# Layer 0 of a four-layer graph network: the x tiles turned on TensorE instead of loaded turned

## The chip, the cores and the metric

The kernel runs on one core of a Trainium2 chip. The metric is the device time of one launch in microseconds (us), as a median of several runs; lower is better.

## The reference

The input x is 128 graphs of 64 nodes with 512 features, in float32; adj is one 64x64 matrix of zeros and ones that all graphs share. Four layers follow one another, each as `x = layernorm(x + layer(x))`. Only layer 0 is touched here:

```python
Wi, Wj = (W[:, :Din], W[:, Din:])
mi = jnp.einsum('bkd,od->bko', x, Wi)
mj = jnp.einsum('bkd,od->bko', x, Wj)
a = adj.astype(x.dtype)
deg = a.sum(axis=1)
out = deg[None, :, None] * (mi + b) + jnp.einsum('ij,bjo->bio', a, mj)
```

Layer 1 is a graph attention with four heads, an output attention and a feed-forward part; layers 2 and 3 are graph attentions with one head.

## The kernel before, in words

The 8192 rows of x are cut into T = 64 tiles of 128 rows, two graphs each. Layer 0 is a first block of the program that runs over the 64 tiles; its result goes to a scratch tensor in HBM, and layer 1, then layers 2 and 3, are later blocks that this change leaves alone.

TensorE contracts over partitions, so x must stand with its features on the partitions. The host hands the kernel x twice: as it is, and a second tensor `in_x_turned` in which each tile is already transposed by blocks of 128x128. SyncE loads both for each tile: `xt` (128 rows by 512 features, two buffers) and `xf`, in the profile `x0f` (features on the partitions, two buffers).

Precision comes from splitting: each float32 operand becomes a high part (cast to fp32r) and a low part (the rest), and each product is three matmuls, high by high, high by low and low by high. For one tile t the engines do this, each in its own fixed order, with semaphores between them:

- ScalarE (ACT): `x_hi(t+1)` casts `xf` into `x0T_hi` (L644); then `wj_hi(t)` (L651) casts the product wj out of PSUM; then `normalise(t-1)` writes the layer's output (L656) and issues its store (L659).
- VectorE (DVE): `x_lo(t+1)` (L698), `xf` minus `x0T_hi`; `wj_lo(t)` (L719); in the first 48 tiles one dot product for the attention vectors of later layers (L727), which needs `v_stage` and `a_pair` from HBM; `z(t)` in two steps (L737, L741); statistics (L284, L291).
- TensorE (PE): `products(t)`: 12 matmuls into `wj_psum`, 12 into `wi_psum`, both through `product` (L47), then 2 into `nb_psum` with the adjacency (L774, L775), which wait for `wj_lo(t)`.
- GpSimd (POOL): `xb(t)` = `xt` + `db` (L607), the small steps of the norm (L295, L298, L302, L307), and between them the splitting of layer 1's weights from `stage` into `big_hi` and `big_lo` (L595, L600), one block for two tiles, loaded from its own DMA queue (L591).
- SyncE (SP): in each step, in this order: at the start of a group of 8 tiles the two loads of `a_pair` (L547), in each even tile that of `v_stage` (L551), then a wait for `xT_lo_ready` and the load of `xf` for tile t+3 (L554), then a wait for `xb_ready` and the load of `xt` for tile t+2 (L558).

At the start SP loads `xf[0]`, the adjacency, the first two pieces of layer 0's weight, the bias, `xf[1]` and both `xt` (L524 to L536). Each further piece of the weight is loaded once DVE has made the low part of an earlier one. The one transpose on PE in layer 0 is that of the adjacency (L779).

Later blocks transpose 128x128 blocks on PE too: `pe_turn` of the head attention (L250), `turn_att` (L1973) and `turn_h1` (L1986), four transposes each, into a PSUM bank.

Of the kernel before, what the change touches and what calls it, by code (L numbers as in the profile page):

```python
# [394 lines left out]
            nc.gpsimd.tensor_tensor(self.shift, self.less, self.rstd, ALU.mult).then_inc(self.shift_ready, 1)  # L395


def gnn_stack_kernel(nc, x, x_turned, adj, W0T, b0, Wh, ah, Wo, ao, w1, b1, w2, b2, gamma, beta,
                     W2, a2s, a2d, W3, a3s, a3d, out):
    B, N, _ = x.shape  # L400
    T = B * N // P
# [13 lines left out]
    with ExitStack() as top:  # L415
# [29 lines left out]
        with ExitStack() as ctx:  # L445
# [3 lines left out]
            def sem(n):  # L449
                return ctx.enter_context(nc.semaphore(n))  # L450

            XR, UN = 2, 4
            GROUP = 2 * KC
            WP = 2
            w0 = (sb("w0_hi", [P, 2 * KC, D], F32R), sb("w0_lo", [P, 2 * KC, D], F32R))
# [3 lines left out]
            a_pair = sb("a_pair", [P, 2, D])  # L459
            v_sums = sb("v_sums", [P, KC, 2])  # L460
            xt = [sb(f"xt{r}", [P, D]) for r in range(XR)]
            xf = [sb(f"x0f{r}", [P, KC, P]) for r in range(XR)]
            xT = [(sb(f"x0T_hi{b}", [P, KC, P], F32R), sb(f"x0T_lo{b}", [P, KC, P], F32R)) for b in range(2)]
            xb = sb("xb", [P, D])
            wj = (sb("wj_hi", [P, D], F32R), sb("wj_lo", [P, D], F32R))
# [6 lines left out]
            deg = sb("deg", [P, 1])  # L472
            adj_T = sb("adj_T", [P, P], F32R)
            db = sb("db", [P, D])
            wj_psum = ctx.enter_context(nc.psum_tensor("wj_psum", [P, D], F32))
            wi_psum = [ctx.enter_context(nc.psum_tensor(f"wi_psum{b}", [P, D], F32)) for b in range(2)]
            nb_psum = [ctx.enter_context(nc.psum_tensor(f"nb_psum{b}", [P, D], F32)) for b in range(2)]
# [1 line left out]
            first_sem = sem("first_of_layer0")  # L479
            norm = Norm(nc, ctx, "n0", shifted=True)  # L480
            loaded = [sem(f"loaded{r}") for r in range(XR)]
            turned_loaded = [sem(f"turned_loaded{r}") for r in range(XR)]
            w0_loaded = [sem(f"w0_loaded{b}") for b in range(2)]
            small_loaded, b0_loaded, w0_hi_ready, w0_lo_ready = (
                sem("small_loaded"), sem("b0_loaded"), sem("w0_hi_ready"), sem("w0_lo_ready"))
            zeros_set, consts_set, adj_ready, setup_step, bd_ready, bd_turned, adj_T_ready = (
                sem("zeros_set"), sem("consts_set"), sem("adj_ready"), sem("setup_step"), sem("bd_ready"),
                sem("bd_turned"), sem("adj_T_ready"))
            xT_hi_ready, xT_lo_ready, wj_done, wj_hi_ready, wj_lo_ready, wi_done, nb_done = (
                sem("x0T_hi_ready"), sem("x0T_lo_ready"), sem("wj_done"), sem("wj_hi_ready"), sem("wj_lo_ready"),  # L490
                sem("wi_done"), sem("nb_done"))
            xb_ready, own_ready, z_ready, x1_ready = sem("xb_ready"), sem("own_ready"), sem("z_ready"), sem("x1_ready")
            big_hi_ready, big_lo_ready = sem("big_hi_ready"), sem("big_lo_ready")
# [5 lines left out]

            def count(t, r):  # L500

                return 16 * (t // XR) + 16 if isinstance(t, int) else 8 * (t - r) + 16

            def turned_rows(t):

                return x_turned[bass.ts(t, P), :].rearrange("p (c n) -> p c n", n=P)

            def groups(eng, step):

# [11 lines left out]

            @block.sync
            def _(sp):
                sp.dma_start(xf[0][:], turned_rows(0)).then_inc(turned_loaded[0], 16)  # L524
                for g in range(2):
                    sp.dma_start(adj_i[g * NODES:(g + 1) * NODES, :], adj).then_inc(small_loaded, 16)
                for k in range(2 * KC // WP):
                    piece = (k * WP + KC) % (2 * KC) * P
                    ge(sp, w0_lo_ready, k - 1)
                    sp.dma_start(w0f[k % 2], W0T[piece:piece + WP * P, :].rearrange("(c p) n -> p c n", p=P)  # L530
                                 ).then_inc(w0_loaded[k % 2], 16)
                    if k == 1:
                        sp.dma_start(db[:], b0.partition_broadcast(P)).then_inc(b0_loaded, 16)
                        sp.dma_start(xf[1][:], turned_rows(1)).then_inc(turned_loaded[1], 16)
                        for r in range(XR):
                            sp.dma_start(xt[r][:], rows(x_rows, r)).then_inc(loaded[r], 16)  # L536
                sp.wait_ge(xT_lo_ready, 1)
                sp.dma_start(xf[0][:], turned_rows(2)).then_inc(turned_loaded[0], 16)

                def step(t, r, q, G):  # L540
                    late = isinstance(G, int) and G >= HEADS
                    if q is not None and r == 0:
                        ge(sp, v_part, 2 * q)
                        for k in range(2):
                            a = ((a2d, a2s), (a3d, a3s))[G - HEADS][k] if late else ah[
                                bass.ds(G, 1), k * D:(k + 1) * D].rearrange("a o -> (a o)")
                            sp.dma_start(a_pair[:, k, :], a.partition_broadcast(P)).then_inc(pair_loaded, 16)  # L547
                    if q is not None and r % 2 == 0:
                        ge(sp, v_part, 2 * q)
                        source = (W2, W3)[G - HEADS][q % KC * P:(q % KC + 1) * P, :] if late else rows(Wh_rows, q)  # L550
                        sp.dma_start(v_stage[:], source).then_inc(v_loaded, 16)  # L551
                    if not isinstance(t, int) or t + 3 < T:
                        sp.wait_ge(xT_lo_ready, t + 2)
                        sp.dma_start(xf[(r + 1) % XR][:], turned_rows(t + 3)  # L554
                                     ).then_inc(turned_loaded[(r + 1) % XR], 16)
                    if not isinstance(t, int) or t + XR < T:
                        sp.wait_ge(xb_ready, t + 1)
                        sp.dma_start(xt[r % XR][:], rows(x_rows, t + XR)).then_inc(loaded[r % XR], 16)  # L558

                groups(sp, step)  # L560
                for b in range(2):
                    sp.wait_ge(x1_out[b], 16 * T // 2)

            @block.gpsimd
            def _(pool):
# [36 lines left out]
                                            ).then_inc(big_lo_ready, 1)  # L602

                def tile(t, r):
                    pool.wait_ge(loaded[r % XR], count(t, r % XR))
                    ge(pool, own_ready, t)
                    nc.gpsimd.tensor_tensor(xb[:], xt[r % XR][:], db[:], ALU.add).then_inc(xb_ready, 1)  # L607

                def two(t, r, q, source, k):

# [20 lines left out]
            @block.scalar  # L631
            def _(act):
                for k in range(2 * KC // WP):
                    first = (k * WP + KC) % (2 * KC)
                    if k == 0:
                        act.wait_ge(turned_loaded[0], 16)
                        nc.scalar.copy(xT[0][0][:], xf[0][:]).then_inc(xT_hi_ready, 1)
                    act.wait_ge(w0_loaded[k % 2], 16 * (k // 2 + 1))
                    nc.scalar.copy(w0[0][:, first:first + WP, :], w0f[k % 2]).then_inc(w0_hi_ready, 1)

                def x_hi(t, b):
                    act.wait_ge(turned_loaded[b], count(t, b))
                    ge(act, wi_done, t - 1)
                    nc.scalar.copy(xT[b][0][:], xf[b][:]).then_inc(xT_hi_ready, 1)  # L644

                def step(t, b, more=True):
                    if more:
                        x_hi(t + 1, 1 - b)
                    act.wait_ge(wj_done, t + 1)
                    ge(act, nb_done, t)  # L650
                    nc.scalar.copy(wj[0][:], wj_psum[:]).then_inc(wj_hi_ready, 1)  # L651

                def normalise(t, b):
                    act.wait_ge(norm.shift_ready, t + 1)
                    ge(act, x1_out[b], 16 * (t // 2) if isinstance(t, int) else 8 * (t - b))
                    nc.scalar.activation(x1[b], z[:], ACT.Identity, scale=norm.rstd[:], bias=norm.shift[:]  # L656
                                         ).then_inc(x1_ready, 1)
                    act.wait_ge(x1_ready, t + 1)
                    act.dma_start(rows(x1_rows, t), x1[b]).then_inc(x1_out[b], 16)  # L659

                step(0, 0)
                step(1, 1)
                normalise(0, 0)
                with act.Fori(1, T // 2 - 1) as g:
                    step(g * 2, 0)
                    normalise(g * 2 - 1, 1)
                    step(g * 2 + 1, 1)
                    normalise(g * 2, 0)
                step(T - 2, 0)
                normalise(T - 3, 1)  # L670
                step(T - 1, 1, False)
                normalise(T - 2, 0)
                normalise(T - 1, 1)

            @block.vector
            def _(dve):
# [18 lines left out]

                def x_lo(t, b):
                    dve.wait_ge(xT_hi_ready, t + 1)
                    nc.vector.tensor_tensor(xT[b][1][:], xf[b][:], xT[b][0][:].bitcast(F32), ALU.subtract  # L698
                                            ).then_inc(xT_lo_ready, 1)

                for k in range(2 * KC // WP):
# [49 lines left out]

            @block.tensor
            def _(pe):
                def products(t, r):
                    b = r % 2
                    pe.wait_ge(xT_hi_ready, t + 1)
# [20 lines left out]
                pe.wait_ge(consts_set, 8)  # L777
                pe.wait_ge(bd_ready, 2)
                nc.tensor.transpose(nb_psum[1][:, 0:P], adj_bd, ident[:]).then_inc(bd_turned, 1)  # L779
                pe.wait_ge(adj_T_ready, 1)  # L780
                for r in range(UN):
                    products(r, r)
                with pe.Fori(1, T // UN - 1) as g:
                    for r in range(UN):
                        products(g * UN + r, r)
                for r in range(UN):
                    products(T - UN + r, r)


# [1313 lines left out]
```

## Time and profile before

| | |
|---|---|
| median of 3 runs | 3167.48 us (3167.32 to 3173.17) |
| the profiled execution's own time | 3173.17 us |
| its span in the profile | 3171.5 us |
| TensorE (PE) busy | 3092.6 us, 98% of the span |
| VectorE (DVE) busy | 2288.8 us, 72% |
| GpSimd (POOL) busy | 2069.8 us, 65% |
| ScalarE (ACT) busy | 1744.6 us, 55% |
| HBM traffic | 77 GB/s over the span |
| last matmul of layer 0 begins | at 404.65 us |

Times in rows are microseconds from the start of the span, unless a column says ns. PE is the matmuls, PEld the weight loads that run beside them; `SPq`, `ACTq` and `POOLq` are the engines' queues where they issue DMAs. A row's idle time stands with what ended it. Matmuls are pipelined: the time that one shows is longer than the distance to the next, so their cost is read from the distance between starts.

### The profile page before, as it was taken

How to read it: one execution, taken by the hardware profiler on the slowest of the kernel's cores; microseconds unless marked ns; L12 is line 12 of the kernel's file. 1: busy time of each engine (PE TensorE's matmuls, PEld its weight loads, DVE VectorE, ACT ScalarE, POOL GpSimd, SP SyncE). 2: the span in 40 equal slices, each digit the busy share in tenths (PEclk: the TensorE clock that was granted, in tenths of full speed). 3: DMA queues.
4: the chain of work that ended last, by engine and by line, in shares of the span. 5: the costliest groups of instructions: out<-in, count | busy, mean ns of one | idle time of the engine just before them, and what ended most of it. 6: DMA issues, size and time to landing. Idle time of an engine off the chain costs nothing.

```text
span 3171.5 us, 64091 instructions
## 1 busy us (share of the span) xinstructions
PE 3092.6 (98%) x19033; PEld 2680.5 (85%) x19033; DVE 2288.8 (72%) x4897; ACT 1744.6 (55%) x4241; POOL 2069.8 (65%) x2797
## 2 busy tenths in 40 slices
PE   8999969999999999999999999998899999999998
PEld 6778848889888988888888888887688888888886
DVE  6777656777767777777777677765787878787785
ACT  3333345555555555555555555543566666666665
POOL 5666665666666666666666666641677777778785
PEclk9999979999999999999999999999999999999998
DMA  6565510111111111111111111113322222222220
GB/s 193 176 183 178 149 47 28 49 38 60 40 56 43 48 52 46 53 42 50 40 60 40 50 50 46 53 40 124 113 87 96 88 94 89 93 92 90 95 87 27
DMA packets 132076, 244.32 MB, mean 77 GB/s; under 512 B 15281, under 2 KB 15281, under 8 KB 132017
## 3 DMA queue, kind: packets, MB, share of 16 engines
q1 hardware_dynamic: 120240, 218.45, 20.9%
q10 hardware_dynamic: 9216, 16.78, 1.6%
q0 software_dynamic: 2560, 8.39, 1.1%
q8 instruction: 26, 0.43, 0.1%
q14 instruction: 34, 0.27, 0.0%
HBM read 159.68 MB, written 83.89 MB: 77 GB/s over the span
## 4 chain that ended last, share of the span: by engine, by line
PE 77%; issue 4%; POOL 3%; DMA 2%; DVE 1%; SPq 0%; ACT 0%; POOLq 0%; ACTq 0%; DVEq 0%
PE wop L1840 21%; PE hp L1826 21%; PE hp L47 10%; PE wop L47 10%; PE agg L1809 4%; PE shared L1848 2%; PE shared L1946 2%; PE agg L1946 2%; DMA xd<-x_scratch 1%; POOL w_first L1077 1%; PE shared L250 1%; PE hp L1973 1%; PE hp L1986 1%; PE smallp L202 1%; POOL g_terms L1154 0%
## 5 line engine op out<-in xcount | busy, mean ns | idle before, releaser
L1077 POOL TENSOR_TENSOR w_first<-xd,v_row 128x512 f32<-128x512 f32 x504 | 716.9, 1435 | 365.5 <-DMA xd<-x_scratch 326.7
L1826 PE MATMUL hp<-yT_hi,big_hi 128*128 128x256 f32 x2048 | 594.9, 290 | 1.0 <-DVE ex L1546 1.0
L1826 PE MATMUL hp<-yT_lo,big_hi 128*128 128x256 f32 x2048 | 579.7, 283 | 0.0
L1826 PE MATMUL hp<-yT_hi,big_lo 128*128 128x256 f32 x2048 | 579.6, 283 | 0.0
L1840 PE MATMUL wop<-big_hi,hT_hi 128*128 128x512 f32 x1024 | 424.3, 414 | 0.0
L1223 ACT ACTIVATE w_first<-w_first 128x512 f32<-128x512 f32 x504 | 316.8, 629 | 163.0 <-POOL w_first L1077 163.0
L1840 PE MATMUL wop<-big_hi,hT_lo 128*128 128x512 f32 x1024 | 402.3, 393 | 0.0
L1840 PE MATMUL wop<-big_lo,hT_hi 128*128 128x512 f32 x1024 | 400.3, 391 | 0.0
L1826 PEld LDWEIGHTS hp<-yT_hi,big_hi 128*128 128x128 f32 x2048 | 392.7, 192 | 7.8 <-issue 1.1
L1826 PEld LDWEIGHTS hp<-yT_lo,big_hi 128*128 128x128 f32 x2048 | 392.9, 192 | 2.9
L1826 PEld LDWEIGHTS hp<-yT_hi,big_lo 128*128 128x128 f32 x2048 | 392.9, 192 | 0.0
L1552 DVE TENSOR_TENSOR hT_lo<-ex,hT_hi 128x512 fp32r<-128x512 f32 x256 | 240.2, 938 | 183.5 <-ACT hT_hi L1243 181.0
L1154 POOL TENSOR_TENSOR g_terms<-x,g_v_row 128x512 f32<-128x512 f32 x256 | 324.8, 1291 | 22.7 <-ACT x L1409 22.5
L1535 DVE TENSOR_TENSOR yT_lo<-agg,yT_hi 128x512 fp32r<-128x512 f32 x256 | 175.8, 687 | 206.8 <-ACT yT_hi L1231 204.7
L1231 ACT CAST yT_hi<-agg 128x512 fp32r<-128x512 f32 x256 | 149.7, 585 | 251.4 <-PE agg L1809 121.9
L1238 ACT ACTIVATE ex<-hp 128x512 f32<-128x512 f32 x256 | 153.0, 598 | 155.2 <-PE hp L1826 154.4
L1840 PEld LDWEIGHTS wop<-big_hi,hT_hi 128*128 128x128 f32 x1024 | 193.4, 189 | 42.5
L1840 PEld LDWEIGHTS wop<-big_hi,hT_lo 128*128 128x128 f32 x1024 | 192.1, 188 | 42.9
L47 PE MATMUL wop<-w_hi,g_agg_hi 128*128 128x512 f32 x512 | 219.5, 429 | 2.1 <-DVE g_agg_lo L1663 2.0
L1840 PEld LDWEIGHTS wop<-big_lo,hT_hi 128*128 128x128 f32 x1024 | 193.2, 189 | 31.9
L1543 DVE TENSOR_SCALAR ex<-ex 128x512 f32<-128x512 f32 x256 | 159.6, 623 | 79.2 <-ACT ex L1238 79.1
L47 PE MATMUL wop<-w_hi,g_agg_lo 128*128 128x512 f32 x512 | 203.6, 398 | 0.0
(206 smaller groups left out, 7852.9 us busy)
## 6 DMA issues: line engine op xcount, KB each, us to landing
x0f<-in_x_turned SPq DMA_DIRECT2D x64, 256.0 KB, 2.6
xt<-in_x SPq DMA_DIRECT2D x64, 256.0 KB, 3.1
x_scratch<-w_first ACTq DMA_DIRECT2D x64, 256.0 KB, 2.4
xa<-x_scratch SPq DMA_DIRECT2D x64, 256.0 KB, 2.7
att_hi_scratch<-att_hi SPq DMA_DIRECT2D x64, 256.0 KB, 2.0
att_lo_scratch<-who SPq DMA_DIRECT2D x64, 256.0 KB, 2.0
att_scratch<-attT SPq DMA_DIRECT2D x64, 256.0 KB, 2.0
att_hi<-att_hi_scratch SPq DMA_DIRECT2D x64, 256.0 KB, 2.8
```

The lines of the kernel that those rows point to most:

```text
L47: ins = nc.tensor.matmul(out, a, b, start=first and c == 0 and q == 0, stop=last and c == n - 1 and q == 2)
L1077: nc.gpsimd.tensor_tensor(terms[:, k % TR, :], xd[:], v_row[:, k, :], ALU.mult).then_inc(terms_ready, 1)
L1154: nc.gpsimd.tensor_tensor(g.terms[:, k, :], x, g.v_row[:, k, :], ALU.mult).then_inc(g.terms_ready, 1)
L1223: nc.scalar.activation(terms[:, k % TR, :], terms[:, k % TR, :], ACT.Identity, accum_out=at.f[:, j, k:k + 1]).then_inc(at.f_ready[j], 1)
L1231: nc.scalar.copy(yT[0][:, side, :, own].rearrange("p c (g n) -> p g c n", g=2), agg[:].rearrange("p g (h c n) -> p h g c n", h=2, c=KC)[:, ...
L1238: nc.scalar.activation(ex[half][:], hp[half][:], ACT.Exp).then_inc(ex_ready, 1)
L1535: nc.vector.tensor_tensor(yT[1][:, side, :, own].rearrange("p c (g n) -> p g c n", g=2), agg[:].rearrange("p g (h c n) -> p h g c n", h=2, ...
L1543: nc.vector.tensor_scalar(ex[half][:], ex[half][:], 1.0, -1.0, ALU.min, ALU.add).then_inc(neg_ready, 1)
L1552: nc.vector.tensor_tensor(hT[1][:, own, :].rearrange("p c n -> p (c n)"), ex[half][:], hT[0][:, own, :].bitcast(F32).rearrange("p c n -> p ...
L1809: ins = nc.tensor.matmul(by_head(agg[:, g, :])[:, :, c, :], xa[j][own, c * P:(c + 1) * P], at.turned[own, j, 2 * q:2 * q + 2, :], start=Tr ...
L1826: ins = nc.tensor.matmul(hp[half][:, s * 2 * P:(s + 1) * 2 * P], a, b, start=c == 0 and i == 0, stop=c == KC - 1 and i == 2)
L1840: ins = nc.tensor.matmul(wop[j][:], a, b, start=h == 0 and c == 0 and i == 0, stop=h == HEADS - 1 and c == KC - 1 and i == 2)
```

## The change

The second input is gone. SP loads only `xt`, now into four buffers (XR = 4). PE turns each tile itself: `turn_x(t)` waits for the load and makes four 128x128 transposes from `xt` into a PSUM buffer `turn`, of which there are two. `turn_x(t+1)` stands ahead of `products(t)` in PE's order; `turn_x(0)` stands after the transpose of the adjacency. ACT's `x_hi` and DVE's `x_lo` read `turn` in PSUM in the place of `xf` in SBUF, and `x_hi` waits for `xT_done`. SP issues the load of `xt` for tile t+4 after `own_ready` of tile t (the first step of z, L737), where it was issued for tile t+2 after `xb_ready` (L607).

```diff
-            XR, UN = 2, 4
+            XR, UN = 4, 4
-            xf = [sb(f"x0f{r}", [P, KC, P]) for r in range(XR)]
+            turn = [ctx.enter_context(nc.psum_tensor(f"turn0{b}", [P, KC, P], F32)) for b in range(2)]
...
-                sp.dma_start(xf[0][:], turned_rows(0)).then_inc(turned_loaded[0], 16)
+                sp.dma_start(xt[0][:], rows(x_rows, 0)).then_inc(loaded[0], 16)
...
-                        sp.dma_start(xf[1][:], turned_rows(1)).then_inc(turned_loaded[1], 16)
-                        for r in range(XR):
+                        for r in range(1, XR):
                             sp.dma_start(xt[r][:], rows(x_rows, r)).then_inc(loaded[r], 16)
-                sp.wait_ge(xT_lo_ready, 1)
-                sp.dma_start(xf[0][:], turned_rows(2)).then_inc(turned_loaded[0], 16)
...
-                    if not isinstance(t, int) or t + 3 < T:
-                        sp.wait_ge(xT_lo_ready, t + 2)
-                        sp.dma_start(xf[(r + 1) % XR][:], turned_rows(t + 3)
-                                     ).then_inc(turned_loaded[(r + 1) % XR], 16)
                     if not isinstance(t, int) or t + XR < T:
-                        sp.wait_ge(xb_ready, t + 1)
+                        sp.wait_ge(own_ready, t + 1)
                         sp.dma_start(xt[r % XR][:], rows(x_rows, t + XR)).then_inc(loaded[r % XR], 16)
...
                 def x_hi(t, b):
-                    act.wait_ge(turned_loaded[b], count(t, b))
+                    act.wait_ge(xT_done, t + 1)
                     ge(act, wi_done, t - 1)
-                    nc.scalar.copy(xT[b][0][:], xf[b][:]).then_inc(xT_hi_ready, 1)
+                    nc.scalar.copy(xT[b][0][:], turn[b][:]).then_inc(xT_hi_ready, 1)
...
-                    nc.vector.tensor_tensor(xT[b][1][:], xf[b][:], xT[b][0][:].bitcast(F32), ALU.subtract
+                    nc.vector.tensor_tensor(xT[b][1][:], turn[b][:], xT[b][0][:].bitcast(F32), ALU.subtract
...
+                def turn_x(t, r):
+                    pe.wait_ge(loaded[r % XR], count(t, r % XR))
+                    ge(pe, xT_lo_ready, t - 1)
+                    for c in range(KC):
+                        ins = nc.tensor.transpose(turn[r % 2][:, c, :], xt[r % XR][:, c * P:(c + 1) * P], ident[:])
+                    ins.then_inc(xT_done, 1)
...
                 nc.tensor.transpose(nb_psum[1][:, 0:P], adj_bd, ident[:]).then_inc(bd_turned, 1)
+                turn_x(0, 0)
                 pe.wait_ge(adj_T_ready, 1)
                 for r in range(UN):
+                    turn_x(r + 1, r + 1)
                     products(r, r)
```

The loop over the middle tiles and the last four tiles have `turn_x(t + 1)` ahead of `products(t)` in the same way; the last tile has nothing to turn ahead.

## Rows read from the trace of the kernel before

**Rows 1.** The page, parts 1 and 2: busy us and share; tenths in 40 slices.
```profile
PE 3092.6 (98%) x19033; PEld 2680.5 (85%) x19033; DVE 2288.8 (72%) x4897; ACT 1744.6 (55%) x4241; POOL 2069.8 (65%) x2797
...
DMA  6565510111111111111111111113322222222220
```

**Rows 2.** Windows: busy us of PE, PEld, DVE, ACT, POOL; PEclk, DMA share, GB/s.
```profile
30.00:400.00 370.00, 367.82 (x1573) 294.51 (x1572) 253.18 (x520) 121.92 (x181) 248.56 (x392) 1.00 0.58 172
```

**Rows 3.** Timeline, layer 0: the first nb matmul of four tiles (start, us).
```profile
18.68 0.40 PE L774 MATMUL nb_psum<-wj_hi,adj_T 128*128 128x512 f32 x1
...
392.29 0.39 PE L774 MATMUL nb_psum<-wj_hi,adj_T 128*128 128x512 f32 x1
...
398.35 0.39 PE L774 MATMUL nb_psum<-wj_hi,adj_T 128*128 128x512 f32 x1
...
404.42 0.39 PE L774 MATMUL nb_psum<-wj_hi,adj_T 128*128 128x512 f32 x1
```

**Rows 4.** Waits, 0 to 410 us: waiter, releaser: us in total, times, longest.
```profile
DVE z L737 <- POOL xb L607: 80.1, 46, 3.0
...
DVE junk L727 <- DMA v_stage<-in_L_gnn_W_heads: 11.7, 5, 3.6
...
PEld nb_psum L774 <- DVE wj_lo L719: 4.8, 7, 1.3
```

**Rows 5.** Timeline, layer 1: four transposes between matmuls on PE.
```profile
1228.97 0.60 PE L250 MATMUL shared<-ident,ah_prob 128*128 128x128 f32 x4
1229.33 0.48 PE L1840 MATMUL wop<-big_hi,hT_hi 128*128 128x512 f32 x1
1229.64 0.39 PE L1840 MATMUL wop<-big_lo,hT_hi 128*128 128x512 f32 x1
1229.87 0.40 PE L1840 MATMUL wop<-big_hi,hT_lo 128*128 128x512 f32 x1
```

**Rows 6.** Source line 1973: duration in ns, min/median/max.
```profile
L1973 PE MATMUL hp<-ident,att x256: 270/272/421, 2197.3 to 3103.5; 128*128 128x128 f32 x128
```

**Rows 7.** Timeline of the start of the kernel.
```profile
3.62 0.62 ACT L637 CAST x0T_hi<-x0f 128x512 fp32r<-128x512 f32 x1 [1.45 <-DMA x0f<-in_x_turned]
...
5.92 0.45 PE L779 MATMUL nb_psum<-ident,z 128*128 128x128 f32 x1 [5.92 <-DVE z L688]
...
6.87 1.04 ACT L639 CAST w_hi<-w_first 128x1024 fp32r<-128x1024 f32 x1 [2.63 <-DMA w_first<-in_L_gnn_W]
...
10.02 0.77 PE L47 MATMUL wj_psum<-w_hi,x0T_hi 128*128 128x512 f32 x1 [3.65 <-DVE x0T_lo L698]
...
17.19 0.50 PE L47 MATMUL wi_psum<-w_hi,x0T_hi 128*128 128x512 f32 x1 [0.35 <-DVE w_lo L704]
```

**Rows 8.** Timeline of tiles 8 and 9, the head of a group.
```profile
64.48 0.33 SPq L551 DMA_DIRECT2D v_stage<-in_L_gnn_W_heads  x1
...
65.79 0.68 DVE L719 TENSOR_TENSOR wj_lo<-wj_psum,wj_hi 128x512 fp32r<-128x512 f32 x1
...
67.21 0.39 PE L774 MATMUL nb_psum<-wj_hi,adj_T 128*128 128x512 f32 x1
...
70.05 0.70 DVE L727 CUSTOM_DVE_ANT_0 junk<-v_stage,a_pair 128x512 f32<-128x512 f32 x1 [3.58 <-DMA v_stage<-in_L_gnn_W_heads]
...
73.61 0.68 DVE L719 TENSOR_TENSOR wj_lo<-wj_psum,wj_hi 128x512 fp32r<-128x512 f32 x1
...
74.35 0.50 PE L774 MATMUL nb_psum<-wj_hi,adj_T 128*128 128x512 f32 x1 [0.91 <-DVE wj_lo L719]
```

**Rows 9.** Lines by form, 40 to 380 us: busy us, mean ns, idle before.
```profile
L737 DVE SCALAR_TENSOR_TENSOR z<-wi_psum,deg,xb 128x512 f32<-128x512 f32 x55 | 41.2, 750 | 74.6 <-POOL xb L607 71.5 <-PE wi_psum L47 3.1
...
L719 DVE TENSOR_TENSOR wj_lo<-wj_psum,wj_hi 128x512 fp32r<-128x512 f32 x56 | 38.3, 685 | 3.7 <-ACT wj_hi L651 3.7
...
L698 DVE TENSOR_TENSOR x0T_lo<-x0f,x0T_hi 128x512 fp32r<-128x512 f32 x56 | 37.9, 677 | 0.7 <-issue 0.7
L644 ACT CAST x0T_hi<-x0f 128x512 fp32r<-128x512 f32 x55 | 34.2, 621 | 45.4 <-ACT w_first L656 37.3 <-PE wi_psum L47 8.1
```

More of the change, by code:

```diff
@@ L395, in pool_rstd, with gnn_stack_kernel @@
             nc.gpsimd.tensor_tensor(self.shift, self.less, self.rstd, ALU.mult).then_inc(self.shift_ready, 1)
-def gnn_stack_kernel(nc, x, x_turned, adj, W0T, b0, Wh, ah, Wo, ao, w1, b1, w2, b2, gamma, beta,
+def gnn_stack_kernel(nc, x, adj, W0T, b0, Wh, ah, Wo, ao, w1, b1, w2, b2, gamma, beta,
                      W2, a2s, a2d, W3, a3s, a3d, out):
@@ L481, in gnn_stack_kernel @@
             loaded = [sem(f"loaded{r}") for r in range(XR)]
-            turned_loaded = [sem(f"turned_loaded{r}") for r in range(XR)]
             w0_loaded = [sem(f"w0_loaded{b}") for b in range(2)]
@@ L488, in gnn_stack_kernel @@
                 sem("bd_turned"), sem("adj_T_ready"))
-            xT_hi_ready, xT_lo_ready, wj_done, wj_hi_ready, wj_lo_ready, wi_done, nb_done = (
-                sem("x0T_hi_ready"), sem("x0T_lo_ready"), sem("wj_done"), sem("wj_hi_ready"), sem("wj_lo_ready"),
+            xT_done, xT_hi_ready, xT_lo_ready, wj_done, wj_hi_ready, wj_lo_ready, wi_done, nb_done = (
+                sem("x0T_done"), sem("x0T_hi_ready"), sem("x0T_lo_ready"), sem("wj_done"), sem("wj_hi_ready"), sem("wj_lo_ready"),
                 sem("wi_done"), sem("nb_done"))
@@ L500, in count @@
             def count(t, r):
-                return 16 * (t // XR) + 16 if isinstance(t, int) else 8 * (t - r) + 16
-            def turned_rows(t):
-                return x_turned[bass.ts(t, P), :].rearrange("p (c n) -> p c n", n=P)
+                return 16 * (t // XR) + 16 if isinstance(t, int) else 4 * (t - r) + 16
             def groups(eng, step):
@@ L604, in tile @@
                 def tile(t, r):
-                    pool.wait_ge(loaded[r % XR], count(t, r % XR))
+                    pool.wait_ge(loaded[r], count(t, r))
                     ge(pool, own_ready, t)
-                    nc.gpsimd.tensor_tensor(xb[:], xt[r % XR][:], db[:], ALU.add).then_inc(xb_ready, 1)
+                    nc.gpsimd.tensor_tensor(xb[:], xt[r][:], db[:], ALU.add).then_inc(xb_ready, 1)
                 def two(t, r, q, source, k):
@@ L635, in _ @@
                     if k == 0:
-                        act.wait_ge(turned_loaded[0], 16)
-                        nc.scalar.copy(xT[0][0][:], xf[0][:]).then_inc(xT_hi_ready, 1)
+                        act.wait_ge(xT_done, 1)
+                        nc.scalar.copy(xT[0][0][:], turn[0][:]).then_inc(xT_hi_ready, 1)
                     act.wait_ge(w0_loaded[k % 2], 16 * (k // 2 + 1))
@@ L779, in _ @@
                 nc.tensor.transpose(nb_psum[1][:, 0:P], adj_bd, ident[:]).then_inc(bd_turned, 1)
+                turn_x(0, 0)
                 pe.wait_ge(adj_T_ready, 1)
                 for r in range(UN):
+                    turn_x(r + 1, r + 1)
                     products(r, r)
                 with pe.Fori(1, T // UN - 1) as g:
+                    t = g * UN
                     for r in range(UN):
-                        products(g * UN + r, r)
+                        if r < UN - 1:
+                            turn_x(t + (r + 1), r + 1)
+                        else:
+                            turn_x(t + UN, 0)
+                        products(t + r, r)
                 for r in range(UN):
+                    if r < UN - 1:
+                        turn_x(T - UN + r + 1, r + 1)
                     products(T - UN + r, r)
@@ L2090 @@
         args.append(nc.dram_tensor(f"in_{name}", a.shape, _mybir.dt.from_np(a.dtype), kind="ExternalInput").ap())
-        if name == 'x':
-            n_rows, width = a.size // a.shape[-1], a.shape[-1]
-            turned = _np.ascontiguousarray(a.reshape(n_rows // P, P, width // P, P).transpose(0, 3, 2, 1)
-                                           .reshape(n_rows, width))
-            arrays["in_x_turned"] = turned
-            args.append(nc.dram_tensor("in_x_turned", turned.shape, _mybir.dt.from_np(turned.dtype),
-                                       kind="ExternalInput").ap())
     shape = inputs['x'].shape
```

## The prediction

> **What bounds the kernel now.** I read the page first. PE is busy for 98% of the span [rows 1], so the question is what the change does to PE's own list of work. The DMA line of the page shows where the loads matter: layer 0 takes the first five of the 40 slices, with DMA at five to six tenths, against one tenth after it [rows 1]. Next I read the windows of layer 0. From 30 to 400 us PE is busy for 367.82 of 370 us at a granted clock of 1.00 (the level of 2.4 GHz), while DVE stands at 253.18, POOL at 248.56 and ACT at 121.92 us [rows 2]. So layer 0 is bound by PE, and PE is without work for about 2 us of it.
>
> Then I looked at PE's beat in the timeline. The first nb matmul of a tile comes 6.06 and 6.07 us after that of the tile before (392.29, 398.35, 404.42), and a tile has 26 matmuls, so one takes 0.233 us. From tile 0 (18.68) to tile 63 (404.42) there are 385.7 us; 63 beats of 6.065 us would be 382.1 [rows 3]. All that PE loses in these tiles is thus 3.6 us. The view of waits agrees in size: the weight load of nb waited seven times for wj_lo, 4.8 us in all [rows 4]. This 3.6 us is the most that any relief of the other engines or of the DMA queues can give back in the steady part.
>
> Where it is lost shows at the head of a group. The dot product of tile 8 waits 3.58 us for v_stage, issued at 64.48, and runs at 70.05; all of DVE's work behind it is late, z and the statistics of tile 8, then wj_lo of tile 9, which runs from 73.61; nb of tile 9 starts at 74.35, 7.14 us after that of tile 8 instead of 6.07 [rows 8].
>
> **The change part by part.** First, *the added transposes*. PE gets 64 times four transposes of 128x128 float32. The kernel has the same operation in layer 1. There the four start at 1228.97, where the next matmul would have started; the matmul behind them starts at 1229.33 and the second one at 1229.64, where without the four it would have been at 1228.97 + 0.23 = 1229.20 [rows 5]. So four transposes cost 0.36 us themselves and 0.08 us at the change back to the wide matmul: 0.44 us. Two of the 64 turns lie in the start, where PE waits anyway (below). 62 x 0.44 = 27.3 us. Bounds: 62 x 0.36 = 22.3 us if the 0.08 is absorbed, and 62 x 0.60 = 37.2 us if the group costs its whole shown length of 0.60 us [rows 5]. I take 27.3, since the beat of the matmuls behind it settles at once (1229.87 is 0.23 after 1229.64). Nothing hides this work: it is put on the engine that has no idle time.
>
> A rule of the Trainium skill would make it dearer. The row first: one such transpose shows a length of 272 ns [rows 6], but four of them let the next matmul start after 0.36 us [rows 5], so they overlap. The Trainium skill (TensorE: Matmul & The Clock Gate, Part 4: PE-mode transpose) gives about 275 ns for one in a kernel; if that were the cost in the queue, 62 x 4 x 0.275 would be an estimated 68 us. The length agrees with the trace, the cost in the queue does not.
>
> Second, *the removed loads*. 64 loads of 256 KB, 16.8 MB, leave SP's queue. No matmul waits for one of them in the steady part: x_hi's idle time ends by ACT's own earlier work or by PE [rows 9]. Their worth is only in what shares the queue, v_stage and stage: at most the 3.6 us above.
>
> Third, *the moved operand*. x_hi and x_lo read PSUM. DVE's other subtraction of that size, wj_lo, already reads PSUM and takes 685 ns, x_lo from SBUF 677 [rows 9]; ACT, with x_hi, is idle two thirds of the time [rows 2]. Cost nothing. The new chain is turn_x(t+1), x_hi, x_lo: about 0.44 + 0.62 + 0.68 = 1.8 us with some 0.1 for each hand-over, 2.1 us from the start of a step of 6.5 us. It ends 4 us before products(t+1) needs it, and before wj_hi(t), the next in ACT's order, which can't start until 12 matmuls are done (0.44 + 2.8 us). If this cover were gone, PE would wait for the rest of the chain in each tile. The wait for xT_lo of tile t-1 in turn_x(t+1) is met a whole step before. Behind turn_x in PE's order stands all of products(t), so a late xt would stop PE; but with four buffers it is issued over two steps ahead.
>
> Fourth, *the load of xt after own_ready*. SP now stands 0.75 us (L737, [rows 9]) longer before it issues xt, and at the head of a group a_pair and v_stage are queued behind it. So v_stage of tile 8 goes out up to 0.75 us later against DVE's work, and the dot product, z and the next wj_lo are late by as much. Against that PE's step is longer by 0.44 us, two steps lie between, and z of the tile before may start earlier (it waits for POOL's xb for 80.1 us in 46 tiles, [rows 4], and POOL gets the same extra 0.44 us in each tile). In tile 9 wj_lo was 1.07 us late; it will be 0 to 0.9 us late. Of the 3.6 us, 0 to 3.6 come back; I take 1.8.
>
> Fifth, *the start*. Today x_hi(0) runs at 3.62, in ACT's idle time before the cast of the first weight piece at 6.87 [rows 7]. It will have to wait for turn_x(0), which stands behind the transpose of the adjacency (5.92 + 0.45): four transposes at the low level of the clock, which I put at 0.7 us from 6.2 on, then x_hi(0) to about 7.6. The weight cast moves from 6.87 to 7.7, and with it DVE's low parts, the first product (10.02) and the later weight pieces, whose loads wait for DVE, up to the last at 17.19 [rows 7]. I take 1.0 us, between 0 (the later pieces are not moved) and 2 us. turn_x(1) falls into PE's wait for x_lo(0).
>
> The sum: 27.3 + 1.0 - 1.8 = 26.5 us. Against the profiled execution's own 3173.17 us that is 3199.7; it stands 5.7 us above the median of the runs shown, and since the change adds work and doesn't scale it, the same 26.5 us on the median of 3167.5 give 3194.0 us. The layers behind see the same work, shifted.
>
> **The rivals.**
> *The transposes cost their length.* 62 x 4 x 0.272 = 67.5 us, and with the other terms 3167.5 + 67.5 + 1.0 - 1.8 = 3234 us. For it: the length in [rows 6]. Against it: the starts in [rows 5].
>
> *The group heads get worse.* v_stage comes later than the longer step can hide: where DVE's lateness grows and POOL's chain follows it, the 3.6 us double instead of halving, and each of six heads may lose 2 us: 27.3 + 1 + 3.6 to 27.3 + 1 + 12, that is 3199 to 3208 us. For it: five waits of up to 3.6 us already stand there [rows 4]. Against: a quarter of the traffic is gone and POOL has slack.
>
> *Faster.* The pace of the matmuls is bound by the traffic into SBUF: 512 columns at 2.4 GHz are 0.213 us and the beat is 0.233. If a quarter less traffic (16.8 MB of some 69, 172 GB/s over 400 us, [rows 2]) gave all of this back, 64 x 26 x 0.02 = 33 us would go: 3161 us. It decides from 0.016 us for each matmul on. Against it: in layer 1, with DMA at one tenth, the beat is 0.23 as well [rows 1, 5].
>
> *It hides.* The transposes fall into waits of PE, within 6 us of today. This needs over 20 us of such waits, and there are 3.6 us [rows 3].
>
> **How the numbers follow.** My forecast has 78 in 100, costly transposes 5, worse group heads 12, faster 2, hidden 3. The forecast's own ends are 22.3 - 3.6 + 0 = 18.7 and 37.2 + 2 = 39.2 us, 3186 to 3207; the range of 3184 to 3205 takes the median's own scatter in (the runs shown differ by 5.9 us), most of the worse heads, and leaves out the full 0.60 us for each group. A change of under 0.2%, 6 us, couldn't be told from none. Faster by more than that: 0.02; within: 0.03; slower: 0.95.
>
> **What would show it.** Right: a beat of 6.50 us between the nb matmuls of neighbouring tiles; four transposes at 0.09 us from start to start and 0.31 us to the second matmul behind; the last nb matmul of layer 0 near 431 us instead of 404.65, and all later blocks shifted by that and otherwise alike; first product near 11 us; DMA share in layer 0 lower by about a quarter. The estimate of the stalls is wrong if the waits of nb for wj_lo are over 3.6 us; the estimate of the transposes is wrong if the beat is over 6.6 or under 6.4; a wait of turn_x for the load of xt, or of products for x_lo, would be a chain that I have left out.

## The result and the profile after

The changed kernel takes 3193.91 us in the median of four runs (3189.90 to 3198.32), the one before 3167.40 us on the same chip (3165.21 to 3173.17). The ratio is 1.0082 with a 95% interval of 1.0062 to 1.0100: slower by 0.8%, 26.5 us, with an interval of 20 to 32 us. Three single runs of the experiments below took two to three times as long as the others (7950.74, 10216.21 and 6149.54 us) and are left out of their medians.

The page of the changed kernel, parts 1 and 2. PE has 256 matmuls more and 22 us more of busy time; DMA in layer 0 stands at three to four tenths, where [rows 1] has five to six:

```profile
PE 3114.8 (98%) x19289; PEld 2703.4 (85%) x19289; DVE 2307.7 (72%) x4897; ACT 1740.2 (55%) x4241; POOL 2040.8 (64%) x2797
...
DMA  4444310111111111111111111113332222222220
```

The same window as in [rows 2]. PE is busy all but 0.9 us; the DMA share falls from 0.58 to 0.40 and the rate from 172 to 124 GB/s:

```profile
30.00:400.00 370.00, 369.14 (x1702) 299.01 (x1701) 264.25 (x494) 108.66 (x170) 208.62 (x369) 1.00 0.40 124
```

A beat below is the time from the first nb matmul of one tile to that of the next. PE in the timeline, the end of tile 0 and the first turn in the steady part, then the first nb matmul of tile 9 and of tile 10, and those of the last two tiles:

```profile
20.23 0.40 PE L769 MATMUL nb_psum<-wj_hi,adj_T 128*128 128x512 f32 x1
20.46 0.39 PE L770 MATMUL nb_psum<-wj_lo,adj_T 128*128 128x512 f32 x1
20.69 0.60 PE L746 MATMUL turn<-ident,xt 128*128 128x128 f32 x4
21.05 0.48 PE L47 MATMUL wj_psum<-w_hi,x0T_hi 128*128 128x512 f32 x1
21.36 0.40 PE L47 MATMUL wj_psum<-w_lo,x0T_hi 128*128 128x512 f32 x1
...
78.73 0.40 PE L769 MATMUL nb_psum<-wj_hi,adj_T 128*128 128x512 f32 x1
...
85.23 0.40 PE L769 MATMUL nb_psum<-wj_hi,adj_T 128*128 128x512 f32 x1
...
424.91 0.40 PE L769 MATMUL nb_psum<-wj_hi,adj_T 128*128 128x512 f32 x1
...
430.98 0.39 PE L769 MATMUL nb_psum<-wj_hi,adj_T 128*128 128x512 f32 x1
```

The pattern of the turn is that of [rows 5]: 0.36 us to the matmul behind it, 0.31 more to the second. The beat is 6.50 us with a turn in it and 6.07 without one (the last). The last nb matmul starts at 430.98 instead of 404.42 [rows 3]: 26.56 us later. That is the size of the difference of the medians; that the two agree to a tenth is partly chance, as the last paragraph of this section shows.

The waits of the changed kernel in layer 0, as in [rows 4]:

```profile
DVE junk L715 <- DMA v_stage<-in_L_gnn_W_heads: 12.0, 6, 4.4
...
DVE z L725 <- POOL xb L595: 8.4, 7, 1.7
...
PEld nb_psum L769 <- DVE wj_lo L707: 2.2, 3, 1.1
```

DVE now waits 8.4 us for xb, where it waited 80.1: the loop of POOL and DVE no longer runs close to PE's beat. The longer beat does most of this by itself, since in the kernel before with only the transposes added (below) the same wait is 23.3 us. nb waits 2.2 us instead of 4.8. In the starts of the nb matmuls, three group heads have longer beats (behind tiles 16, 24 and 32), 1.7 us in all over the beat of 6.50; in the kernel before it was 3.6 us.

Lines by form, 40 to 400 us, of the changed kernel; to be read against [rows 9]:

```profile
L715 DVE CUSTOM_DVE_ANT_0 junk<-v_stage,a_pair 128x512 f32<-128x512 f32 x45 | 62.8, 1396 | 17.8 <-DMA v_stage<-in_L_gnn_W_heads 12.0 <-DMA v_stage<-in_L_gnn_W 5.3 <-issue 0.5
...
L686 DVE TENSOR_TENSOR x0T_lo<-turn,x0T_hi 128x512 fp32r<-128x512 f32 x55 | 37.1, 674 | 0.7 <-issue 0.7
...
L632 ACT CAST x0T_hi<-turn 128x512 fp32r<-128x512 f32 x55 | 32.4, 588 | 120.8 <-PE turn L746 120.8
...
L295 POOL TENSOR_TENSOR n_veps<-n_mv,norm_consts 128x1 f32<-128x1 f32 x55 | 10.5, 191 | 91.6 <-DVE n_mv L291 91.2
```

x_lo and x_hi cost from PSUM no more than from SBUF (674 against 677 ns, 588 against 621). The small POOL operation n_veps takes 191 ns on average; in the same window of the kernel before it took 552:

```profile
L295 POOL TENSOR_TENSOR n_veps<-n_mv,norm_consts 128x1 f32<-128x1 f32 x59 | 32.6, 552 | 53.1 <-DVE n_mv L291 53.0
```

One number must not be read from the spans alone. The spans differ by 18.3 us, the medians by 26.5. From the last nb matmul of layer 0 to the end of the span the kernel before has 3171.5 - 404.4 = 2767.1 us and the changed one 3189.8 - 431.0 = 2758.8, for identical work. Over the ten profiled executions of this study that remainder lies between 2758.7 and 2767.1 us; the one of before is the longest of them. So one pair of profiled executions can't settle a few microseconds of the whole time; the medians and the beats of layer 0 can.

### The profile page after: what moved, and what is told of

Same layout as the page of the kernel before. It is cut to its first block, busy times and chain, and to the rows that moved or that the text cites. A ratio compares the mean times of both kernels' runs of the same rounds, so it can differ in the third digit from the quotient of the medians.

```text
span 3189.8 us, 64591 instructions
## 1 busy us (share of the span) xinstructions
PE 3114.8 (98%) x19289; PEld 2703.4 (85%) x19289; DVE 2307.7 (72%) x4897; ACT 1740.2 (55%) x4241; POOL 2040.8 (64%) x2797
## 4 chain that ended last, share of the span: by engine, by line
PE 78%; issue 3%; POOL 3%; DMA 1%; DVE 1%; ACT 0%; SPq 0%; POOLq 0%; ACTq 0%; DVEq 0%
PE wop L1844 21%; PE hp L1830 21%; PE hp L47 10%; PE wop L47 10%; PE agg L1813 4%; PE shared L1852 2%; PE shared L1950 2%; PE agg L1950 2%; POOL w_first L1081 1%; DMA xd<-x_scratch 1%; PE shared L250 1%; PE hp L1977 1%; PE hp L1990 1%; PE smallp L202 1%; POOL g_terms L1158 0%
```

## The experiments

Each kernel below was run on the same chip as runs of the kernel before, in two sessions: 11 runs of before beside turns added, turned twice, old loads and before with the dot product last, 21 beside the other four, with a median of 3168.79 us in both. Kernels of different sessions are best compared by their ratios to before. I use three measures: the time, the start of the first nb matmul of tile 0, and the 63 beats from there to that of tile 63, which are free of the scatter of the later layers. Without stalls and turns 63 beats take 382.1 us.

| kernel | time, median | ratio to before, 95% | first nb | 63 beats |
|---|---|---|---|---|
| before | 3168.79 | | 18.68 | 385.7 |
| changed | 3193.91 | 1.0082 (1.0062 to 1.0100) | 20.23 | 410.8 |
| before, turns added | 3192.90 | 1.0081 (1.0068 to 1.0094) | 20.21 | 409.5 |
| changed, turned twice | 3223.01 | 1.0171 (1.0158 to 1.0184) | 19.80 | 436.8 |
| changed, with the old loads | 3195.33 | 1.0084 (1.0071 to 1.0097) | 19.77 | 412.9 |
| before, xt after own_ready | 3175.94 | 1.0021 (1.0012 to 1.0030) | 18.50 | 389.7 |
| before, v_stage early | 3168.04 | 0.9997 (0.9988 to 1.0006) | 19.58 | 382.6 |
| before, dot product last | 3190.78 | 1.0068 (1.0055 to 1.0081) | 19.97 | 406.5 |
| changed, dot product last | 3192.76 | 1.0078 (1.0064 to 1.0092) | 20.05 | 409.1 |
| changed, start reordered | 3196.24 | 1.0091 (1.0077 to 1.0104) | 19.49 | 411.0 |

(The changed kernel's row is from its own session, beside four runs of before with a median of 3167.40.)

### The transposes alone, put into the kernel before

The transposes write a PSUM buffer `turn`, allocated for them, that nobody reads:

```diff
                 def products(t, r):
                     b = r % 2
+                    if not isinstance(t, int) or 0 < t < T - 1:
+                        for c in range(KC):
+                            nc.tensor.transpose(turn[b][:, c, :], ident[:], ident[:])
                     pe.wait_ge(xT_hi_ready, t + 1)
```

> The kernel before, with all its loads, and in each of the tiles 1 to 62 four more 128x128 float32 transposes ahead of the products on PE (of ident, into a PSUM buffer that nobody reads). Theory (the cost is PE's own work): the beat of the nb matmuls goes from 6.07 to 6.50 us, the last nb matmul from 404.4 to 428 to 431 us, the time 24 to 27 us over before; the start is as before, first product at 10.0 us. Rival (the cost is in the new chain of load, turn, cast, or in the changed order of the loads): the beat stays under 6.2 us and the time within 6 us of before. POOL's n_veps (0.55 us before, 0.19 us after) stays at 0.55 us if it was x_lo's reading of two SBUF tiles that held it, since x_lo is unchanged here; it falls if it was only the longer beat.

Measured: 24 us over before, a ratio of 1.0081, the same as the whole change. PE of this kernel, then its last nb matmul:

```profile
20.67 0.60 PE L759 MATMUL turn<-ident 128*128 128x128 f32 x4
21.03 0.48 PE L47 MATMUL wj_psum<-w_hi,x0T_hi 128*128 128x512 f32 x1
21.34 0.39 PE L47 MATMUL wj_psum<-w_lo,x0T_hi 128*128 128x512 f32 x1
...
429.67 0.39 PE L778 MATMUL nb_psum<-wj_hi,adj_T 128*128 128x512 f32 x1
```

63 beats take 429.67 - 20.21 = 409.46 us and nb waits for wj_lo nowhere. (409.46 - 382.1) / 62 = 0.441 us for each four. The cost of the change is PE's own work: with all loads, all casts and the order of the queues as before, it is there in full. The stalls vanish by the longer beat alone, all 3.6 us of them, while the changed kernel keeps 1.7. And n_veps stays slow, as its row in the lines by form shows:

```profile
L295 POOL TENSOR_TENSOR n_veps<-n_mv,norm_consts 128x1 f32<-128x1 f32 x55 | 30.2, 550 | 67.0 <-DVE n_mv L291 66.5
```

### Every tile turned twice

```diff
-                    for c in range(KC):
-                        ins = nc.tensor.transpose(turn[r % 2][:, c, :], xt[r % XR][:, c * P:(c + 1) * P], ident[:])
+                    for k in range(2 if not isinstance(t, int) or t > 1 else 1):
+                        for c in range(KC):
+                            ins = nc.tensor.transpose(turn[r % 2][:, c, :], xt[r % XR][:, c * P:(c + 1) * P], ident[:])
```

> The changed kernel, where each tile from 2 to 63 is turned twice into the same buffer. Theory: the second four cost only their start-to-start distance, 0.36 us, since the change back to wide matmuls (0.08 us) is already paid: beat 6.86 us, 62 x 0.36 = 22 us over the changed kernel. Rival 1: every four cost 0.44 us: 27 us. Rival 2: a transpose costs its shown length, 0.272 us each: 67 us.

Measured: 29 us over the changed kernel (3223.01 against 3193.91; 28 us by the two ratios). My theory was wrong here and rival 1 right. In the timeline the eight transposes and the two matmuls behind them:

```profile
75.84 1.04 PE L747 MATMUL turn<-ident,xt 128*128 128x128 f32 x8
76.63 0.48 PE L47 MATMUL wj_psum<-w_hi,x0T_hi 128*128 128x512 f32 x1
76.95 0.40 PE L47 MATMUL wj_psum<-w_lo,x0T_hi 128*128 128x512 f32 x1
```

Eight take 0.79 us to the next start, four took 0.36: the second four cost 0.43. Over the layer: (436.75 - 382.1) / 62 = 0.881 us for eight, twice 0.441; the changed kernel's own undisturbed beat, 6.50 against 6.065, gives 0.435 for four. So the cost is 0.11 us for each transpose, in proportion to their number. There is no separate price for going back to wide matmuls: the first matmul behind the group starts early and its successor makes up for it.

### The old loads put back into the changed kernel

The main part of the edit; the rest hands the kernel the second input again and gives it an SBUF tile that nobody reads:

```diff
+                    if not isinstance(t, int) or t + 3 < T:
+                        sp.wait_ge(xT_lo_ready, t + 2)
+                        sp.dma_start(xf[:], x_turned[bass.ts(t + 3, P), :].rearrange("p (c n) -> p c n", n=P)
+                                     ).then_inc(spare_loaded[(r + 1) % 2], 16)
```

ACT's x_hi also waits for the landing of the load of one step before, so that the loads into the one buffer keep their order.

> The changed kernel, which also loads the turned tiles as before (61 loads of 256 KB into an SBUF tile that nobody reads). Theory (the removed loads were worth nothing but a little of the stalls): DMA share in layer 0 back from 0.40 to near 0.58, the time within 3 us of the changed kernel, the beat 6.50 us. Rival (less traffic gave several us back, and the transposes cost more than I read): 5 to 15 us over the changed kernel. POOL's n_veps stays at 0.19 us if it is x_lo's operand that holds it, and goes back towards 0.55 us if it was the traffic.

Measured: 3195.33 us, 1.4 over the changed kernel, within the scatter of both; 63 beats take 2.2 us more, and nb waits 4.5 us instead of 2.2. ACT's x_hi waited 33.7 us for these loads, a wait that only this kernel has, so the 2.2 us are an upper bound rather than a clean price. Its window and its n_veps:

```profile
30.00:400.00 370.00, 367.23 (x1691) 297.03 (x1690) 262.64 (x491) 108.48 (x170) 207.92 (x368) 1.00 0.53 163
```

```profile
L295 POOL TENSOR_TENSOR n_veps<-n_mv,norm_consts 128x1 f32<-128x1 f32 x55 | 10.4, 189 | 85.3 <-DVE n_mv L291 85.2
```

The loads (61 of the 64) were worth some 2 us of beats at most. The longer beats stand at four group heads (behind tiles 8, 16, 24 and 32), where v_stage is awaited: the dot product waits for it 24.5 us in all instead of 17.3. And n_veps stays at 189 ns with the traffic back, while it stayed at 550 ns without the change of x_lo's operand.

### The new order of SP's queue, alone, on the kernel before

```diff
-                        sp.wait_ge(xb_ready, t + 1)
+                        sp.wait_ge(own_ready, t + 1)
```

> The kernel before, where SP waits for own_ready instead of xb_ready ahead of each load of xt: this part of the change alone, with nothing of the longer beat. Theory (v_stage behind it goes out 0.75 us later and DVE is late by as much): the stalls of nb grow from 3.6 to 5 to 9 us, the time 1 to 5 us higher. Rival (it is hidden): within 1 us, as the landing of v_stage and not its issue decides.

Measured: 7 us over before (4 to 10 by the interval); the profiled execution has 63 beats of 389.7 us, 7.6 us of stalls instead of 3.6. The stalls lie within the 5 to 9 us expected; the time moved by more than the 1 to 5 us expected, though its interval reaches into that range. Its waits:

```profile
DVE junk L727 <- DMA v_stage<-in_L_gnn_W_heads: 19.2, 13, 4.4
...
PEld nb_psum L774 <- DVE wj_lo L719: 8.6, 6, 2.2
```

This part of the change has a price of its own, where the beat of PE gives no room: 4.0 us in the beats of layer 0. In the changed kernel the beat is 0.44 us longer and most of the price is not paid. The 1.7 us that it still stalls at group heads may be the rest of it, since the kernel with the old order and the turns added stalls nowhere; the changed kernel with the old order was not run.

### v_stage issued early in the kernel before

SP issues a_pair and v_stage for the next two tiles one step earlier, ahead of the wait for xb_ready. The main part of the edit; `stage_loads` holds the old lines that issue them:

```diff
+                    if r % 2 == 1 and not (isinstance(G, int) and t + 1 >= (HEADS + 2) * GROUP):
+                        if r < GROUP - 1:
+                            stage_loads(G * KC + (r + 1) // 2, False, G)
+                        else:
+                            stage_loads((G + 1) * KC, True, G + 1)
                     if not isinstance(t, int) or t + XR < T:
                         sp.wait_ge(xb_ready, t + 1)
```

> The kernel before, where SP issues a_pair and v_stage of the next pair of tiles in the step before, ahead of its wait for xb_ready, as soon as DVE is done with the old ones. Theory (the 3.6 us of stalls in the steady part come from v_stage at the head of a group): the longest wait of the dot product falls from 3.6 to under 2 us, nb waits for wj_lo under 1 us in all, 63 beats take 382 to 383 us instead of 385.7, the time 2 to 4 us lower. Rival (POOL's chain makes the stalls): no change.

Measured: 63 beats of 402.13 - 19.58 = 382.55 us; the stalls are gone but for 0.45 us, and with them the wait of nb:

```profile
PEld nb_psum L787 <- DVE wj_lo L732: 0.9, 3, 0.4
```

So the 3.6 us did come from v_stage. The time did not move as expected (ratio 0.9997, 0.9988 to 1.0006, that is 4 us less to 2 us more): 3 us of 3168 are at the edge of what these runs resolve, and the first nb matmul of this execution happened to be 0.9 us later. It is no proven improvement over the kernel before.

### The dot product last, in both kernels

DVE's wait for the pair and the dot product behind it move below z and its statistics (shortened):

```diff
-                    if q is not None:
-                        dve.wait_ge(pair_loaded, pairs(q, r))
...
                     norm.dve_stats(nc, dve, t, z[:])
                     norm.dve_mean(nc, dve, t, x1_ready)
+                    if q is not None:
+                        dve.wait_ge(pair_loaded, pairs(q, r))
```

> The kernel before, with DVE's dot product (and its wait for v_stage) behind the statistics of z instead of ahead of z. Theory (the stalls of nb in the steady part come from that wait): the waits of nb for wj_lo vanish, the last nb matmul is 3 us earlier, near 401 us, and the time 2 to 4 us lower. Rival: the dot product now delays x_lo and wj_lo of the next tile instead, or v_stage is loaded too late: last nb matmul at 404 us or later.

Measured on the kernel before: 22 us slower (17 to 26 by the interval), where I had expected 3 us less. 63 beats take 406.5 us. One step of it in the timeline, DVE and POOL:

```profile
102.48 0.70 DVE L738 CUSTOM_DVE_ANT_0 junk<-v_stage,a_pair 128x512 f32<-128x512 f32 x1
102.49 0.73 POOL L295 TENSOR_TENSOR n_veps<-n_mv,norm_consts 128x1 f32<-128x1 f32 x1 [0.15 <-DVE n_mv L291]
...
103.10 0.69 DVE L698 TENSOR_TENSOR x0T_lo<-x0f,x0T_hi 128x512 fp32r<-128x512 f32 x1
103.18 0.65 POOL L298 TENSOR_TENSOR n_less<-n_mv,norm_consts 128x1 f32<-128x1 f32 x1
103.70 0.68 DVE L719 TENSOR_TENSOR wj_lo<-wj_psum,wj_hi 128x512 fp32r<-128x512 f32 x1
...
104.44 0.50 PE L774 MATMUL nb_psum<-wj_hi,adj_T 128*128 128x512 f32 x1 [0.69 <-DVE wj_lo L719]
104.58 1.30 POOL L607 TENSOR_TENSOR xb<-xt,db 128x512 f32<-128x512 f32 x1
```

POOL's n_veps ends with the dot product (103.22 and 103.18), n_less with x_lo (103.83 and 103.79). Both push xb back, which z waits for (120.8 us in layer 0 instead of 80.1), and the dot product now stands between z and the next wj_lo. nb waits for wj_lo 32 times. The two causes are not told apart. From the start of n_veps to that of xb, POOL takes only 0.3 us longer on average (2.5 us instead of 2.2, between 40 and 320 us), because n_shift is shorter now (0.22 us instead of 0.45) and gives part back; the beat of the 48 tiles is 0.5 us longer. So what POOL loses explains about half, and that the new place of the dot product makes up the rest is argued, not shown.

> The changed kernel with DVE's dot product behind the statistics of z, the same edit that cost the kernel before 22 us. Theory (there the dot product and x_lo, two DVE operations with both inputs in SBUF, ran back to back over POOL's n_veps and n_less, 0.7 and 0.65 us instead of 0.2 each, and the loop of POOL and DVE became longer than PE's beat): here x_lo reads PSUM, n_less stays at 0.19 us, and the beat of 6.50 us has room, so the beat stays at 6.50 and the time within 3 us of the changed kernel. Rival (the dot product ahead of wj_lo is what made wj_lo late): nb waits 10 us or more here too, 10 to 20 us over the changed kernel.

Measured on the changed kernel: the same edit costs nothing. 63 beats take 409.06 us, the stalls are zero, the time is 3192.76 us against 3193.91, which is no difference. Its rows of n_less and n_veps, duration min/median/max in ns:

```profile
L298 POOL TENSOR_TENSOR n_less<-n_mv,norm_consts x64: 181/186/195, 23.4 to 432.0; 128x1 f32<-128x1 f32 x64
```

```profile
L295 POOL TENSOR_TENSOR n_veps<-n_mv,norm_consts x64: 184/626/734, 22.8 to 431.9; 128x1 f32<-128x1 f32 x64
```

n_less, beside an x_lo that reads PSUM, is short; n_veps, beside the dot product, is long again. The two runs don't tell apart how much of the harmlessness is this and how much the longer beat.

### The start reordered in the changed kernel

ACT casts the first weight piece ahead of x_hi(0); PE makes turn_x(1) between the two products of tile 0. PE's part of the edit:

```diff
-                for r in range(UN):
-                    turn_x(r + 1, r + 1)
-                    products(r, r)
+                products(0, 0, between=lambda: turn_x(1, 1))
+                for r in range(1, UN):
```

> The changed kernel with its start reordered: ACT casts the first weight piece ahead of x_hi(0), and PE makes turn_x(1) between the wj and the wi products of tile 0, not ahead of both. Theory 1 (my fifth step: x_hi(0) and turn_x(1) delay the start by about 1 us): first product near 10.0 us instead of 11.6, first nb matmul near 19 instead of 20.2, time 1 us lower. Theory 2 (since the kernel before with transposes added had its first nb matmul at 20.2 too: the start is bound by the landing of the third weight piece, whatever PE and ACT do): first product earlier, first nb matmul still at 19.5 to 20.3, time unchanged.

Measured: first product at 10.30 us, first nb matmul at 19.49, time 3196.24 us, not lower. The first product moves by 1.3 us, the first nb matmul by 0.7 against the changed kernel and by 0.3 against the lowest of the four executions with turned tiles (19.77 to 20.23, below). Theory 2 fits the time better; a gain of half a microsecond can't be excluded.

## Why the prediction was right, point by point

**The bound.** PE's own list of work set the time of layer 0, and the added work came through in full. The transposes alone, in the kernel before, gave the same ratio as the whole change (1.0081 and 1.0082). The 3194.0 us forecast and the 3193.91 measured agree to 0.1 us, where the measured difference has an interval of 20 to 32 us: that closeness is luck. The terms:

| term | forecast | measured |
|---|---|---|
| 62 turns | 27.3 us (0.44 each) | 27.0 us (0.435 each, from the undisturbed beats of the changed kernel; 27.3 in the kernel with turns added) |
| stalls given back | -1.8 | 410.75 - 27.0 - 382.1 leaves 1.7 of 3.6: -1.9 |
| start | +1.0 | +1.55 between the two profiled executions |
| sum | 26.5 | 26.6 |

**The added transposes.** The sum was right and its split wrong. I read 0.36 us of transposes and 0.08 us for the change back to wide matmuls; the doubled turn shows 0.11 us for each transpose and no second price. My lower bound of 62 x 0.36 was therefore no possible value, and the upper one, the shown length, was none either. The 275 ns of the Trainium skill (TensorE: Matmul & The Clock Gate, Part 4: PE-mode transpose) agree with the shown length, a median of 272 ns in the changed kernel too, and 0.11 us is what one costs in the queue.

**The removed loads.** Worth at most 2.2 us of beats, as the kernel with the old loads shows; I had bounded this by 3.6 us. The rival that the matmuls would run faster with less traffic is refuted: the beat with a turn is 6.50 us with DMA at 0.40 and with DMA at 0.53 or 0.56 (old loads, turns added), and the one without a turn is still 6.07 us.

**The moved operand.** "Cost nothing" held: 674 and 588 ns. What I missed is that it shortens a POOL operation. In the lines by form n_veps falls from 552 to 191 ns, and the two controls tell the reason: 550 ns with the longer beat and x_lo from SBUF, 189 ns with the old traffic and x_lo from PSUM. The Trainium skill (GPSIMD Engine Reference, 8. Key points) says that GpSimd shares its SBUF interfaces with VectorE and contends with DVE instructions that have two SBUF inputs. The traces agree: x_lo had two and now has one. The gain hides behind PE here.

**The load of xt after own_ready.** The mechanism that I priced is real: alone it costs the kernel before 4.0 us of beats and 7 us of time (4 to 10). In the changed kernel the longer beat covers most of it: of the 3.6 us of stalls 1.9 came back, where I took 1.8. In the kernel with turns added all 3.6 came back.

**The start.** This term is the weak one. The first product did move, from 10.02 to 11.57 us, and by more than I took for the term: over the profiled executions it lies at 9.13 to 10.02 us with the old start and at 11.39 to 11.57 with turned tiles in the changed kernel's order. The rows of the changed kernel's start show why, one step of it unforeseen: turn_x(1) does not fall into PE's wait for x_lo(0) but waits for the load of xt[1], and takes 1.09 us, ahead of the first product. I had put this stretch at the low level of the clock. The matmuls there do start 0.43 us apart (12.57 and 13.00) instead of 0.23, but the granted clock of the window reads 1.00, so the low level is not shown by the profile:

```profile
6.64 0.59 ACT L625 CAST x0T_hi<-turn 128x512 fp32r<-128x512 f32 x1 [4.47 <-PE turn L746]
...
10.84 1.09 PE L746 MATMUL turn<-ident,xt 128*128 128x128 f32 x4 [4.24 <-DMA xt<-in_x]
...
11.57 0.78 PE L47 MATMUL wj_psum<-w_hi,x0T_hi 128*128 128x512 f32 x1
...
12.57 0.63 PE L47 MATMUL wj_psum<-w_hi,x0T_lo 128*128 128x512 f32 x1
...
13.00 0.63 PE L47 MATMUL wj_psum<-w_hi,x0T_hi 128*128 128x512 f32 x1
...
13.36 1.05 ACT L627 CAST w_hi<-w_first 128x1024 fp32r<-128x1024 f32 x1 [4.25 <-DMA w_first<-in_L_gnn_W]
```

But the kernel with the turns added has the start of the kernel before and still its first nb matmul at 20.21 us. Its row for the third weight piece shows the wait that decides:

```profile
13.41 1.05 ACT L640 CAST w_hi<-w_first 128x1024 fp32r<-128x1024 f32 x1 [4.71 <-DMA w_first<-in_L_gnn_W]
```

Over the five executions with the old start the first nb matmul lies at 18.50, 18.68, 19.58, 19.97 and 20.21 us, over the four with turned tiles and the changed kernel's start at 19.77 to 20.23. The means differ by 0.6 us (19.39 and 19.96), less than the scatter of 1.7 us. What the change costs in the start is between nothing and 1.5 us; these runs don't settle it further.

**The rivals.** Costly transposes (3234 us) and hidden transposes fell with the beat of 6.50 us. Worse group heads (3199 to 3208) did not come, since nb waits less, not more, than before.

## What to carry to other kernels

Where an engine is busy for 99% of a stretch, a change there is priced by that engine's list alone: count what it adds, take the distance between starts where the same operation already stands in the trace (0.11 us a transpose here, not its shown 0.27), and leave the other engines only the few microseconds that the bound engine idles. Loading an input that the host has laid out already cost little here (at most some 2 us for 61 loads of 256 KB), and the work that replaces it on the bound engine costs its full price. Before an in-order engine's operations are rearranged to save a small stall, look at who runs beside each of them: the same reordering cost 22 us in one kernel and nothing in the other.

## What the runs showed of the hardware that I had not expected

- The 128x1 POOL operations n_veps and n_less take 0.19 us beside a DVE operation with one SBUF and one PSUM input (x_lo in the changed kernel), and 0.55 to 0.73 us beside one with two SBUF inputs: they end within 0.05 us of the DVE operation.
- DVE pays as well. Its dot product of two SBUF tiles takes about 0.70 us with no wide POOL operation beside it (both kernels with the dot product last, mean 700 and 701 ns) and 1.35 to 1.40 us on average in the changed kernel and in the one with turns added, where the phase of the beat puts it beside POOL's 128x512 operations. In the changed kernel that is 31 us of DVE time more from 40 to 400 us, and nb still waits only 2.2 us.
- Four 128x128 float32 transposes show 1.06 to 1.09 us in the start, where the matmuls behind them ran at 0.43 us from start to start, and 0.60 us in the steady part, where they ran at 0.23; the granted clock of both stretches reads 1.00.
- In ten profiled executions the identical later layers took between 2758.7 and 2767.1 us, which is as much as a third of the effect under study. Undisturbed beats of the changed layer agree to a hundredth of a microsecond.
